# A four-layer graph network on one core: batched strips, a reordered edge loop, and weights scaled in the sort

## Time and profile before

| | us |
|---|---|
| median of 3 runs (2803.76 to 2804.41) | 2804.22 |
| the profiled execution | 2801.62 |
| its span | 2799.8 |

### The profile page before, as it was taken

The page is one execution under the profiler, slowest core; times in us unless marked ns, Lnnn a source line. Parts: engine busy times, 40 slices in busy tenths (PEclk is TensorE's granted clock), DMA queues, the critical chain, the costliest instruction groups (busy, mean ns, idle before and its releaser), DMA issues. The chain is left out here.

```text
span 2799.8 us, 70675 instructions
## 1 busy us (share of the span) xinstructions
PE 2212.1 (79%) x26560; PEld 1628.7 (58%) x26560; DVE 1636.7 (58%) x4376; ACT 1368.2 (49%) x3156; POOL 1532.0 (55%) x1701
## 2 busy tenths in 40 slices
PE   0428787788727999999999967999999859995895
PEld 0103333333316888888888854666666559995773
DVE  5825444444405666666666656999999835552001
ACT  1005333333316888887888856888888600000110
POOL 2007777777756777777777734888888700000000
PEclk9967666656558999999999987999999969998997
DMA  8874444444330433343333425777777340007856
GB/s 352 363 288 112 113 113 114 113 114 113 109 89 16 163 120 118 118 157 125 117 118 118 163 102 153 199 192 200 199 192 200 94 83 3 3 3 313 334 228 288
DMA packets 252686, 427.70 MB, mean 153 GB/s; under 512 B 128564, under 2 KB 214222, under 8 KB 242725
## 3 DMA queue, kind: packets, MB, share of 16 engines
q1 hardware_dynamic: 194630, 337.86, 34.0%
q0 software_dynamic: 54800, 83.75, 12.3%
q10 hardware_dynamic: 2924, 1.57, 0.2%
HBM read 233.42 MB, written 209.72 MB: 158 GB/s over the span
## 5 line engine op out<-in xcount | busy, mean ns | idle before, releaser
L331 POOL DMA_INDIRECT sorted_edges<-s_records,s_index x400 | 476.3, 1191 | 311.5 <-issue 307.9
L803 POOL TENSOR_TENSOR e_ohw<-e_oh,e_rec 128x512 bf16<-128x512 bf16 x314 | 474.3, 1530 | 4.9 <-DVE e_oh L1056 4.9
L1524 PE MATMUL m_p_acc<-m_prod,m_oh 128*128 128x344 f32 x1250 | 400.6, 464 | 33.4 <-DVE m_prod L1585 22.6
L1524 PEld LDWEIGHTS m_p_acc<-m_prod,m_oh 128*128 128x128 f32 x1250 | 226.2, 191 | 148.1 <-issue 56.2
L1566 DVE TENSOR_TENSOR m_prod<-m_rec,m_coef 128x256 f32<-128x256 f32 x471 | 233.3, 546 | 0.0
L809 POOL TENSOR_TENSOR e_part<-e_rest,e_part 128x256 bf16<-128x256 f32 x157 | 104.0, 662 | 226.6 <-ACT e_part L871 226.6
L859 ACT ACTIVATE e_ohw<-e_oh,e_rec 128x128 bf16<-128x128 bf16 x628 | 216.2, 394 | 0.0
L1056 DVE TENSOR_TENSOR e_oh<-e_iota,e_rec 128x1024 bf16<-128x1024 f32 x157 | 212.2, 1353 | 0.2 <-DVE e_w_parts L91 0.2
L1782 PE MATMUL q_p_next<-q_g,pair 128*128 128x96 bf16 x4725 | 202.3, 207 | 0.0
L1782 PEld LDWEIGHTS q_p_next<-q_g,pair 128*128 128x128 bf16 x4725 | 201.3, 98 | 0.0
L1073 DVE COPY e_strip<-e_p_aw 128x512 f32<-128x512 f32 (+1 forms) x325 | 200.6, 660 | 0.0
(11 more groups left out here) (347 smaller groups left out, 4904.3 us busy)
## 6 DMA issues: line engine op xcount, KB each, us to landing
dense_strips<-e_strip SPq DMA_DIRECT2D x25, 3200.0 KB, 10.0
pair<-dense_strips SPq DMA_DIRECT2D x49, 1600.0 KB, 19.0
m_rec<-sorted_edges SPq DMA_DIRECT2D x138, 526.0 KB, 3.9
sorted_edges<-s_neg SPq DMA_DIRECT2D x5, 12560.0 KB, 68.5
pair<-dense_strips POOLq DMA_DIRECT2D x25, 800.0 KB, 8.9
e_rec<-sorted_edges SPq DMA_DIRECT2D x156, 108.0 KB, 2.3
sorted_edges<-s_records,s_index POOLq DMA_INDIRECT x400, 3.9
m_rec<-sorted_edges SPq DMA_DIRECT2D x12, 394.5 KB, 3.9
```

The lines of the kernel that those rows point to most:

```text
L331: pool.indirect_dma_start(dram["edges"], bass.IndirectOffsetOnAxis(ap=index[u % RING][:, c:c + 1], axis=0), record[u % RING][:, c, :], Non ...
L803: i = g_.tensor_tensor(ohw[g % 4][:, :, k, :], oh[s][:, :, 0, :], rec[s][:, :, c:c + 1].to_broadcast([P, G, P]), ALU.mult)
L1524: i = mm(p_acc[d % 2][:, 0:TERMS], oh[g % 4][:, t % G, :], prod[g % 3][:, t % G, :], start=(t % NB == 0), stop=(t % NB == NB - 1), skip_gr ...
```

## The change

1. **Sort**: the eviction multiplies W00 and W10 by the edge's sh0 as it copies them, and stores W10 and W01 interleaved in runs of eight.
2. **Setup of loop 1**: the 18 transfers of weights move from ScalarE's queue to SP's, behind the first two record loads; the memsets come before the tables; the cut of the weights comes at table 3; the first six one-hot groups are made between the last tables.
3. **Loop 1**: `turn` is split; the one-hots are transposed first, the records after them; ScalarE copies in that order. Record slots are released by the records' transposes.
4. **Loop 2**: `scale` and `coef` go; DVE and POOL read `node` and the new layout.
5. **Nodes, layer 2**: the degree stage and the norms move into the second node stage. POOL asks for strips 18 to 24 there, all at once. TensorE waits for the first 21 strips, and for the last four when it reaches the 22nd. SP fetches `stacked` at the start of layer 2.
6. **Layer 3**: ties go to the slot that was freed first, so the loads of pass 3 wait for 51, 52, and so on up to 62 finished steps. Four strips form a batch with one PSUM bank, one copy by ScalarE (up to 512 columns), four turning products in a row and one copy by DVE.

```diff
@@ sort_phase, evict
-                    i = nc.scalar.copy(record[u % RING][:, c:c + 2, CT:REC], p_w[half][0:EP, :, :])
+                    to, of = (whole.rearrange("p c (r k u) -> p c r k u", k=2, u=MUL)
+                              for whole in (record[u % RING][:, c:c + 2, CT:REC], p_w[half][0:EP, :, :]))
+                    for k in range(2):
+                        e = u * UC + c + k
+                        nc.scalar.activation(to[:, k, :, 0, :], of[:, k, :, 0, :], ACT.Copy, scale=tail[:, e, C4 - CW:C4 - CW + 1])
+                    i = nc.scalar.copy(to[:, :, :, 1, :], of[:, :, :, 1, :])
@@ layer0_edges_phase, SP, ScalarE, TensorE, DVE
             for g in range(2):
                 load(g)
+            sp.wait_ge(setup, 1)
+            for k, (wn, name) in enumerate(((1, "f"), (0, "b"))):
...
             for g in range(2, U):
                 load(g)
...
-                staged(j, (middle, 2), (copy_rec, 5), (copy_oh, 5), (weigh_first, 4), (relu1, 4), (weigh_last, 4), (relu2, 3))
+                staged(j, (middle, 2), (copy_oh, 5), (copy_rec, 5), (weigh_first, 4), (relu1, 4), (weigh_last, 4), (relu2, 3))
...
-                staged(j, (turn, 5), (hidden, 4), (second, 3), (sums, 1), (dense, 2))
+                staged(j, (turn_one_hots, 5), (turn_records, 5), (hidden, 4), (second, 3), (sums, 1), (dense, 2))
...
+            for i in range(TABLES):
...
+                if i == 3:
+                    dve.wait_ge(d_b, 288)
+                    cut_weights(dve, V, w_chain, w1e[:, :, :].rearrange("p k h -> p (k h)"), w1_parts)
+                if i >= TABLES - READY:
+                    one_hots(i - (TABLES - READY))
@@ layer1_edges_phase
+        def lower(record):
+
+            return record[:, :, RT + 2 * MM:RT + 4 * MM].rearrange("p t (w u) -> p t w u", w=MUL)
...
-            def scale(g):
-                made_prod.before(pool, g, 3)
...
-                staged(j, (dot_products, 4), (scale, 4), (dot_sum, 4), (direct_products, 4), (dot_total, 4))
+                staged(j, (dot_products, 4), (dot_sum, 4), (direct_products, 4), (dot_total, 4))
...
-                                        rec[g % SLOTS][:, :, RT + 3 * MM:RT + 4 * MM].rearrange("p t (w u) -> p t w u", w=MUL),
-                                        coef[g % 3][:, :, k * MUL:(k + 1) * MUL].unsqueeze(2).to_broadcast([P, G, MUL, MUL]), ALU.mult)
+                                        lower(rec[g % SLOTS])[:, :, :, 0:MUL],
+                                        node[g % 4][:, :, k * MUL:(k + 1) * MUL].unsqueeze(2).to_broadcast([P, G, MUL, MUL]), ALU.mult)
@@ nodes_phase, layer2_phase
-                bring_counts(pool, dram, keep["A"], range(EARLY, EARLY + MORE))
+                bring_counts(pool, dram, keep["A"], range(EARLY, NB))
...
-                pe.wait_ge(a_loaded, 16 * NB)
+                pe.wait_ge(a_loaded, 16 * SOON)
...
+                        if u == 0 and b == SOON:
+                            pe.wait_ge(dram["a_late"], 16 * (NB - SOON))
@@ layer3_phase
-                    k = holds.pop(max(later, key=lambda c: later[c]))
+                    k = holds.pop(max(later, key=lambda c: (later[c], -freed[holds[c]])))
...
+            def turn(m):
+                pe.wait_ge(copied, m + 1)
+                if m >= 4:
+                    pe.wait_ge(gathered, m - 3)
+                for k in range(len(batches[m])):
+                    i = nc.tensor.matmul(p_t[m % 4][:, D * k:D * k + D], sT[m % 2][:, k, :], stacked[:, :], start=True, stop=True, skip_group_check=True)
+                i.then_inc(turned, 1)
```

More of the change, by code:

```diff
@@ L54 @@
 EARLY, MORE = 18, 3
+SOON = EARLY + MORE
 HELD = -(-NB // 2)
@@ L899, in _, with turn_one_hots, turn_records @@
             pe.wait_ge(cleared, 4)
-            def turn(g):
+            def turn_one_hots(g):
+                s = g % U
+                onehots.after(pe, g)
+                ohT_copied.before(pe, g, 1)
+                pe.sem_inc(prime, 1)
+                for k in range(2):
+                    for t in range(G):
+                        i = nc.tensor.transpose(p_oh[:, k, t, :], oh[s][:, t, k, :], identb[:, :])
+                turned.set_by(i)
+            def turn_records(g):
                 s = g % U
@@ L1027, in _ @@
             V.memset(w2[:, :, :], 0.0).then_inc(setup, 1)
-            for i in range(TABLES):
-                n, to, y = table(i)
-                tab_hi.after(dve, i)
-                tab_low.before(dve, i, 2)
-                dve.sem_inc(prime, 1)
-                tab_cut.set_by(V.tensor_tensor(tab_rest[i % 2][:, 0:n, :], y, to[:, :, 0, :], ALU.subtract))
             for s in range(4):
@@ L1224, in _ @@
                 i.then_inc(s_t, 1)
+            if layer == 1:
+                pe.wait_ge(s_most, 1)
+                for k in range(2):
+                    i = nc.tensor.matmul(p_row[:, k, :], most[:, k:k + 1], ident[:, :], start=True, stop=True, skip_group_check=True)
+                i.then_inc(s_row, 1)
             pe.wait_ge(s_w, 16 * loads)
@@ L1329, in layer1_edges_phase @@
         ohT = ring("ohT", [P, G * P], 2, BF16)
-        node = ring("node", [P, G, D], 4)
-        coef = ring("coef", [P, G, SE], 3)
+        node = ring("node", [P, G, SE], 4)
         dots = ring("dots", [P, G, 3, MUL], 2)
@@ L2060, in _, with place @@
             sp.wait_ge(stored, 16)
+        batches, batch_at = [], {}
+        for n in range(STEPS3):
+            for c in range(0, NB, BATCH):
+                for i in range(c, min(c + BATCH, NB)):
+                    batch_at[n, i] = len(batches)
+                batches.append(order[n][c:c + BATCH])
+        def place(m, b):
+            return sorted(batches[m]).index(b)
         @block.tensor
         def _(pe):
-            def turn(q):
-                pe.wait_ge(copied, q + 1)
-                if q >= 4:
-                    pe.wait_ge(gathered, q - 3)
-                nc.tensor.matmul(p_t[q % 4][:, 0:D], sT[q % 2][:, :], stacked[:, :], start=True, stop=True).then_inc(turned, 1)
-            pe.wait_ge(d_stacked, 16)
-            for q in range(len(turns)):
+            def turn(m):
[5 more added lines that the diff above has]
+                i.then_inc(turned, 1)
+            pe.wait_ge(dram["d_stacked"], 16)
+            for q, b in enumerate(turns):
                 n = q // NB
+                m = batch_at[n, q % NB]
+                first = b == batches[m][0]
                 features = (x, X[0], X[1])[n]
```

197 lines of the change are left out of this document (89 added, 108 removed).

## The result

The changed kernel takes 2783.99 us (median of 6 runs, 2780.57 to 2794.71) against 2804.6 of the kernel before in the same session (6 runs, 2803.76 to 2805.86): a ratio of 0.9926, interval 0.9913 to 0.9939. It is faster, by 20.6 us, not by the 122 of the forecast. The profiled execution took 2783.01 us, its span is 2781.0; before, the span was 2799.8.

The account below looks back on a forecast made before the run. Loop 1 was taken as bound by a ring of waits between TensorE and DVE, loop 2 by DVE. Terms -9 (setup), -54, -20 (loops), -14 (propagation), -25 (last layer) sum to -122: 2804 to 2682 us, 8-in-10 range 2652 to 2735.

Parts of the forecast that it names:

- Sort: Sort evictions: ScalarE's added work, at most 3.0 us per unit, fits under its 4.8 us wait for slots; cost 0.
- Setup: Setup of loop 1: tables start some 8 us earlier and one-hots behind them go; -9 us, ends -2 and -15.
- some +7 for the stop and the tiles: Setup of loop 1: cost of DVE stopping at table 3 for the weights and of one-hot tiles between tables.
- a sign of being wrong: Setup of loop 1: DVE held at table 3 for over 10 us would show the prediction wrong.
- Loop 1: First edge loop: transposing one-hots first removes TensorE's wait for DVE; -54 us, ends -60 and -20.
- Then TensorE's own work decides: First edge loop: with the ring of waits shortened to 4.59 us, TensorE's work sets the period at 4.66 us.
- another ring: Rival, first edge loop: ScalarE's work and hand-overs keep the period near 4.9 us; 2719 us in all, chance 0.12.
- Loop 2: Second edge loop: removing POOL's scaling frees DVE's three multiplications, 3.28 to 3.13 us per group; -20 us, ends -5 and -32.
- Start of the propagation: Propagation after the second node stage: earlier norms and strip fetches let TensorE start sooner; -14 us, ends -9 and -16.
- I leave 1.4 of them for the change of block: Start of the propagation: of 6.2 us between last node operation and L1830, 1.4 remain, an estimate; -4.8 us.
- Last layer: Layer 3: earlier constant 7 us, third pass 15.5, batches of four strips 2.5; -25 us, ends -15 and -30.
- the forecast 15.5: Last layer, pass 3: loads no longer queued behind the last step, so it runs 61 us instead of 76.6.

Follow-up runs that it names:

- e8_cut_late: e3_spaced with DVE cutting the weights behind table 9 instead of table 3 in the setup of loop 1: 2706.12 us, ratio 0.9647.
- e5_split_strips: e3_spaced with the last four of POOL's seven strips asked for one stage later, as before the change: 2709.59 us, ratio 0.9656.
- e1_old_order: Changed kernel with the old order in loop 1, records transposed and copied before the one-hots: 2746.59 us, ratio 0.9791.
- e3_spaced: Changed kernel with each strip stored in five pieces of 0.64 MB, each as soon as its five tiles are copied: 2711.78 us, ratio 0.9678.

## Why the prediction was wrong

*Sort.* Right at 0. POOL's 400 stores again take 1193 ns with 0.30 us of issue, the last ends at 807.4, and ScalarE waits less for slots: 177.0 us instead of 210.7.

```profile
L337 POOL DMA_INDIRECT sorted_edges<-s_records,s_index x400 | 477.2, 1193 | 311.2 <-issue 307.7
L295 ACT ACTIVATE s_records<-s_p_w,s_tail 125x128 f32<-125x128 f32 x400 | 127.1, 379 | 98.1 <-PE s_p_w L388 97.9
```

*Setup.* -4.6 for -9. The step that was mis-sized is "some +7 for the stop and the tiles": the stop alone is 10.56 us, which the prediction had named as a sign of being wrong. Without it (e8_cut_late) the first hidden product is 8.8 us ahead of before.

*Loop 1.* **The step that failed is "Then TensorE's own work decides".** The ring went as described: no wait for DVE, one-hots first, a period of 4.69 us for the forecast 4.66, and no wait for ScalarE's record copy, so the rival that was priced (another ring) did not come. But a period is not yet a loop. A TensorE that never waited was held up by the arrival of its instructions beside the strip stores: 23 stops, 58.1 us, and 20 to 25 us of clock. This input of the engine was in none of the terms and in none of the rivals. The end of the range allowed only -20 here; it was +36.

Could it have been seen? Yes, in the kernel before, in its last layer. These rows are from its order of time (one strip is 50 products of L2084 in the profile):

```profile
2604.04 1.28 PE L2084 MATMUL r_p_o<-pair,x 128*32 128x128 f32 x35 [1.44 <-issue]
2611.02 0.63 PE L2084 MATMUL r_p_o<-pair,x 128*32 128x128 f32 x13 [1.96 <-issue]
2617.62 1.50 PE L2084 MATMUL r_p_o<-pair,x 128*32 128x128 f32 x44 [1.10 <-issue]
```

TensorE never waits there either, the transfers run at 420 GB/s, and it stops for 1 to 2 us about every 6.5 us, 15.3 us in all. These 13 stops lie a multiple of 256 instructions apart as well, to within one, and each ends 2.3 to 2.6 us after the start of a packet. From 2708 to 2732, while the transfers rest, it does not stop once. I read passes 1 and 2 as undisturbed by their transfers, from their lengths, and never asked what "issue" meant beside full DMA engines.

*Loop 2.* -27.4 for -20. The mechanism was right, and the three multiplications measured as taken (1.52 to 1.36 us). Too small was the term, which counted only them: the outer product L1585 lay beside POOL too. On the page that spoke here, the Trainium skill (SBUF — State Buffer, Who interferes with whom): by its lock the loop was to gain 31 us, and the measurement is nearer to that than to my 20. It does not bear out that the removed operation's whole length comes back: 0.58 us went from POOL, 0.18 came back to DVE. Nor does TensorE alone bound the loop: it is busy for 479.8 of the 488.6 us, DVE still for 486.6.

*Start of the propagation.* -2.7 for -14. The part that failed is "I leave 1.4 of them for the change of block": the stretch between the last node operation and the first of the propagation measured 14.88 us. The packets of the seven strips ended at 2281.0 for the forecast 2279; but moved into the node stage, the fetch held the end of that stage. With three strips there (e5_split_strips) it measured 1.59 us, so the 1.4 would have held for the block alone. I had followed what waits for the strips, and not what waits for POOL.

*Last layer.* -6.8 for -7 in the constant. Passes of 62.8, 62.2 and 62.5 us, where before they were 62.1, 59.8 and 78.9: the third gained 16.4 for the forecast 15.5, and transfers run from its start. The 15.5 are closer than their working: the row at 2708.38 that the prediction took for the start of pass 3 is its second strip, the pass began at 2706.1 and ran 78.9 us, and 61 would have given 17.9. The batches' 2.5 are not seen; in this profile the first two passes are 3 us longer, inside the spread told above. Stops by late instructions are now in all three passes, 26 us instead of 15, and 8.5 of them in the third: part of its 20 us of waits for strips came back as that.

```profile
2703.00:2767.00 64.00, 54.58 (x1310) 49.86 (x1309) 2.31 (x9) 4.05 (x8) 0.00 (x0) 0.89 0.75 310
```

The account: from the forecast's -122 to the measured -18.8 it is +90 from loop 1, +11 from the propagation's start, +5 each from setup and last layer (with its constant), -7 from loop 2. e1_old_order and e3_spaced show that without the instruction stops the rest of the change is worth 55 us, and with the loop's gain 90.

## What to carry to other kernels

Before a wait is taken from the busiest engine, ask what it will live on: in a kernel written out in full, TensorE also needs its instructions, and they come over the same DMA engines as the data. Look for idle time put down to issue where transfers are dense, and send large stores in pieces spread over the loop. And when a transfer is moved ahead into another stage, count what waits for the end of that stage, not only what waits for the data.

## What I had not expected of the hardware

TensorE's instructions arrive in packets of 16,384 bytes, 256 instructions each, and in loop 1 it executed the first of them 2.2 us after the start of the packet at the earliest (2.15 is the least in thirteen traces). Beside a store of 3.2 MB (11 us) a packet comes up to 16 us after the one before, and TensorE stops; with the same bytes in pieces of 0.64 MB the longest stop falls from 4.7 to 1.2 us. The Trainium skill (Runtime: NRT & Kernel Launch, Instruction fetch mechanics) has the blocks of 16 KiB and 256 instructions, which agrees; it calls the cost of crossing a block mostly hidden, and in loop 1 of the changed kernel it was 58 us of stops and, by the estimate above, 20 to 25 us of lower clock.

In loop 1 of the changed kernel the granted clock fell from 2.4 to 1.2 GHz for a while at 14 of the 18 stops of over 2 us, so they cost about 0.4 of their length again. Three stretches around the stop of 3.54 us that ended at 911.14, in the changed kernel:

```profile
875.00:900.00 25.00, 24.77 (x365) 22.09 (x368) 17.30 (x29) 20.78 (x48) 18.70 (x16) 1.00 0.15 29
900.00:925.00 25.00, 20.95 (x271) 18.55 (x273) 14.24 (x22) 15.75 (x37) 14.65 (x12) 0.86 0.40 148
925.00:950.00 25.00, 21.80 (x311) 19.01 (x314) 16.58 (x27) 19.94 (x46) 18.93 (x16) 1.00 0.45 158
```

With stops of at most 1.2 us (loop 1 of e3_spaced) the clock stays at 1.00. In the last pass of the changed kernel (0.89 above) it fell twice, behind stops of 2.05 and 2.12 us.

A block with transfers of POOL's ended 2 us after their last packet, 15 us after the last work in it. What makes it wait is not shown.
